# The first projection right after the first chunk's states, with the tiles of the other chunks in its rounds

## The reference, cut to what matters

```python
x = x + attn(cond(x, itok, W), ...)           # x: 32 x 64 x 1024, so 2048 tokens of 1024
x = x + ffn(cond2(x, ...), ...)
# cond:  states[b] = W[itok[b]].T @ x[b]       W: 16 matrices of 64 x 64, one picked for each of 32 sequences
# attn:  q, k, v = states @ ((qw - 8) * repeat(scales, 128, axis=0))     q: 32 heads, k and v: 8, of 128
#        rotary embedding of q and k, causal softmax, context, output projection (also 4-bit weights)
# cond2: two small layers with weights picked by session; ffn: a dense layer + top-2 of 8 low-rank experts
```

## Time and profile before

| | us |
|---|---|
| median of 3 runs | 1913.29 (1912.41 to 1917.9) |
| the profiled execution: its time | 1915.91 |
| its span | 1913.9 |
| TensorE busy | 1729.1 (90%) |
| VectorE busy | 1598.4 (84%) |
| ScalarE busy | 1407.5 (74%) |

### The profile page before, as it was taken

One profiled execution on the slowest core, in us unless ns is written; L12 is line 12 of the kernel. 1 busy time (PEld: TensorE's weight loads), 2 busy tenths in 40 slices (PEclk: granted clock), 3 DMA queues, 4 the chain that ended last, 5 costly groups with the idle time before them and its releaser, 6 DMA issues. The chain is left out here.

```text
span 1913.9 us, 38885 instructions
## 1 busy us (share of the span) xinstructions
PE 1729.1 (90%) x14314; PEld 937.1 (49%) x14314; DVE 1598.4 (84%) x2715; ACT 1407.5 (74%) x2372; POOL 61.3 (3%) x50
## 2 busy tenths in 40 slices
PE   3668999998999899999999998999999978899998
PEld 3424545554554445445544554554544545455553
DVE  5589999999899898989998998899999987556642
ACT  2557988888898888888888888898888775233420
POOL 0200000000000000000000000000000011111100
PEclk8789999999999999999999999999999999899999
DMA  6321030011102010301021012102013111100001
GB/s 212 101 88 46 12 67 23 24 34 47 46 2 72 9 46 1 78 3 46 14 66 29 20 36 45 46 2 74 5 55 101 52 50 55 67 23 34 23 34 44
DMA packets 118582, 87.66 MB, mean 46 GB/s; under 512 B 11996, under 2 KB 110692, under 8 KB 118372
## 3 DMA queue, kind: packets, MB, share of 16 engines
q1 hardware_dynamic: 117732, 84.76, 14.9%
q10 hardware_dynamic: 640, 0.13, 0.0%
HBM read 76.49 MB, written 8.39 MB: 44 GB/s over the span
## 5 line engine op out<-in xcount | busy, mean ns | idle before, releaser
L1311 ACT ACTIVATE pj<-pj,ratio 128x512 f32<-128x512 f32 x865 | 575.4, 684 | 120.0 <-PE pj L1645 114.6
L1643 PE MATMUL pj<-hid,wts 128*128 128x512 f16 x1024 | 392.8, 384 | 66.8 <-DVE pj L826 25.0
L1645 PE MATMUL pj<-hid,wts 128*128 128x512 f16 x1024 | 390.9, 382 | 0.0
L1320 ACT ACTIVATE sbk<-sbk,wts 128x512 f32<-128x512 f32 x384 | 261.8, 682 | 24.2 <-PE sbk L1712 18.9
L1320 ACT ACTIVATE sa<-sa,wts 128x512 f32<-128x512 f32 x384 | 260.8, 679 | 15.6 <-PE sa L1712 15.5
L1643 PEld LDWEIGHTS pj<-hid,wts 128*128 128x128 f16 x1024 | 99.8, 97 | 235.8 <-ACT pj L1311 71.3
L1655 PEld LDWEIGHTS tp<-wts,hid 128*128 128x128 f16 x3072 | 181.7, 98 | 32.5 <-issue 3.5
L1655 PE MATMUL tp<-wts,hid 128*128 128x128 f16 x3072 | 192.5, 219 | 0.5
L1645 PEld LDWEIGHTS pj<-hid,wts 128*128 128x128 f16 x1024 | 100.7, 98 | 77.3 <-issue 1.4
L726 DVE SCALAR_TENSOR_TENSOR work<-pj,ratio,cos_t 128x512 f32<-128x512 f32 x128 | 95.7, 748 | 44.5 <-PE pj L1645 35.5
L1311 ACT ACTIVATE ex<-ex,ratio 128x512 f32<-128x512 f32 x193 | 127.9, 663 | 4.1 <-PE ex L1645 1.6
(11 more groups left out here) (247 smaller groups left out, 3090.4 us busy)
## 6 DMA issues: line engine op xcount, KB each, us to landing
wts<-qo_d SPq DMA_DIRECT2D x64, 256.0 KB, 3.2
y<-x_d SPq DMA_DIRECT2D x7, 2048.0 KB, 7.8
wts<-qq_d SPq DMA_DIRECT2D x35, 256.0 KB, 3.2
int_even<-qq_d SPq DMA_DIRECT2D x29, 256.0 KB, 3.0
out_d<-y SPq DMA_DIRECT2D x12, 512.0 KB, 2.6
work<-qv_d SPq DMA_DIRECT2D x16, 256.0 KB, 7.7
work<-sv_d SPq DMA_DIRECT2D x16, 256.0 KB, 9.4
work<-wb_d SPq DMA_DIRECT2D x8, 512.0 KB, 4.1
```

The costliest lines, as they stand in the source:

```text
L1311: act.activation(unit_bank[u][:, :], unit_bank[u][:, :], ACT.Copy, scale=ratio[:, KT * u + j:KT * u + j + 1]).then_inc(u_scaled[u], 1)
L1320: act.activation(out_bank[t % 2][:, :], out_bank[t % 2][:, :], ACT.Copy, scale=o_ratio[:, REP * t + h:REP * t + h + 1]).then_inc(o_scaled[ ...
L1643: mm(bank[:, :], w_int[:, u, j, :], hid[:, 0, j, CH * c:CH * (c + 1)], start=j == 0, stop=False, skip_group_check=True)
L1645: mm(bank[:, :], w_int[:, u, j, :], hid[:, 1, j, CH * c:CH * (c + 1)], start=False, stop=True, skip_group_check=True).then_inc(u_done[u], 1)
```

## The change

The states of chunk 0 are made as before (its eighth tile in the bank `cx0`, not in a `pj`). Then the 24 rounds of the first projection start, and each holds one tile of the states of the other chunks: round r has tile 8 + r, so chunk 1 stands in rounds 0 to 7, chunk 2 in 8 to 15, chunk 3 in 16 to 23. These tiles go round in four banks (`cx1`, `sa`, `sbk`, `cx0`), since the units hold the other three. ScalarE has the high half behind the rescales of the round, and its integer conversions spread over rounds; two dequantizing operations stand in round 10. VectorE has in the rounds: the low half, maximum and scale of chunk 2 at round 5 and of chunk 3 at round 13, the ropes of three units at rounds 8, 12 and 16, the dequantizing at round 10, and four maxima of w_base at rounds 20 to 23; the fourth rope, the score factors and the other maxima come behind. The maximum of chunk 1 now stands behind the low halves of chunk 0 and the ratios. SP loads the four small tables right after x of chunk 1, and the value weights after the integers of chunk 1. VectorE waits for the small tables at round 8, TensorE after the rounds.

```diff
@@ -318,12 +318,11 @@
             return ((lambda part: w2h[:, part, :], w2_t, col(SC2 + 2)),
                     (lambda part: wrh[:, part, :, :].rearrange("p k e -> p (k e)"), small[:, 256:320], col(SC2 + 1)))
-        cond_banks = [pj[0], pj[1], ex, cx[0], cx[1], sa, sbk]
-        cond_banks = [pj[0], pj[1], ex, cx[0], cx[1], sa, sbk]
+        cond_first = [pj[0], pj[1], ex, cx[0], cx[1], sa, sbk, cx[0]]
+        cond_later = [cx[1], sa, sbk, cx[0]]
         def cond_bank(n):
-            return cond_banks[n % len(cond_banks)]
+            return cond_first[n] if n < KT else cond_later[n % 4]
         def ctx_src(e):
             return cx[e][:, :].rearrange("p (m s) -> p m s", s=SEQ)
@@ -423,12 +422,13 @@
                     load_x(c + 1)
                 if c == 0:
                     load_scales(0)
+                    for dst, src in ((cos_t, rope_cos), (sin_t, rope_sin), (mask_t, neg_mask), (id16, ident16)):
+                        sp.dma_start(dst[:, :], src).then_inc(S["consts_in"], 16)
+                if c < len(INT_BATCHES):
+                    load_first_ints(c)
+                if c == 1:
                     load_piece(0, 0)
                     load_piece(0, 1)
-                if c < len(INT_BATCHES):
-                    load_first_ints(c)
-            for dst, src in ((cos_t, rope_cos), (sin_t, rope_sin), (mask_t, neg_mask), (id16, ident16)):
-                sp.dma_start(dst[:, :], src).then_inc(S["consts_in"], 16)
             load_out_scales(0)
             load_wo(0, 0)
             load_wo(0, 1)
@@ -649,27 +649,22 @@
             dve.wait_ge(S["w_scales_ready"], 1)
             chunk_max(0)
             chunk_scale(0)
-            for c in range(NC):
-                for k in range(KT):
-                    n = c * KT + k
-                    if k == (KT // 4 if c == 0 else 0) and c + 1 < NC:
-                        chunk_max(c + 1)
-                    dve.wait_ge(S["cond_hi"], n + 1)
-                    t = slice(CH * c, CH * (c + 1))
-                    dve.scalar_tensor_tensor(out=hid[:, 1, k, t], in0=cond_bank(n)[:, :], scalar=col(SH + c),
-                                             in1=hid[:, 0, k, t], op0=ALU.mult, op1=ALU.subtract).then_inc(S["cond_split"], 1)
-                if c == 0:
-                    scales_inverted(0)
-                    unit_ratios(0, 0, 3)
-                    unit_ratios(0, 3, NU)
-                if c + 1 < NC:
-                    chunk_scale(c + 1)
-                if c == 0:
-                    dequant_scale(0, 0)
-                    dequant_scale(0, 1)
-                    dequant_split(0, 0)
-                    dequant_split(0, 1)
+            def cond_lo(n):
+                c, k = n // KT, n % KT
+                t = slice(CH * c, CH * (c + 1))
+                dve.wait_ge(S["cond_hi"], n + 1)
+                dve.scalar_tensor_tensor(out=hid[:, 1, k, t], in0=cond_bank(n)[:, :], scalar=col(SH + c),
+                                         in1=hid[:, 0, k, t], op0=ALU.mult, op1=ALU.subtract).then_inc(S["cond_split"], 1)
+            for n in range(KT):
+                cond_lo(n)
+            scales_inverted(0)
+            unit_ratios(0, 0, 3)
+            unit_ratios(0, 3, NU)
+            chunk_max(1)
+            chunk_scale(1)
             def score_factors():
                 link(dve.tensor_scalar(col(A, NC), col(ISH, NC), 1.0 / QKV_DOWN, None, ALU.mult))
@@ -967,8 +962,6 @@
                 dve.wait_ge(S["base_done"], n + 1)
                 dve.scalar_tensor_tensor(out=x1_part(n), in0=base_bank[n % 2][:, :], scalar=col(F_BASE + n // YT), in1=x1_part(n),
                                          op0=ALU.mult, op1=ALU.add).then_inc(S["result"], 1)
-            dve.wait_ge(S["consts_in"], 64)
             def step(p4, ahead, out4, between, pieces):
@@ -1172,17 +1165,41 @@
                     else:
                         step((g, c), (g, c + 1) if c + 1 < NC else (g + 1, 0), None if first and c == 0 else (g, c - 1), between, pieces)
-            score_factors()
-            for u in range(NU - 1):
+            def first_rope(u):
                 rope_cos((0, 0), u)
                 rope_sin((0, 0), u)
                 rope_add((0, 0), u)
                 if u in (0, 1, 2):
                     rope_high((0, 0), u)
                 rope_split((0, 0), u)
-                for k in (2 * u, 2 * u + 1):
-                    dve.wait_ge(wb_in[k % 2], 16 * (k // 2 + 1))
-                    absmax(wbmax[:, k:k + 1], wb_stage[k % 2]).then_inc(S["wb_read"], 1)
+            def wb_max(k):
+                dve.wait_ge(wb_in[k % 2], 16 * (k // 2 + 1))
+                absmax(wbmax[:, k:k + 1], wb_stage[k % 2]).then_inc(S["wb_read"], 1)
+            for r in range(ROUNDS):
+                if r == 8:
+                    dve.wait_ge(S["consts_in"], 64)
+                cond_lo(KT + r)
+                if r == 5:
+                    chunk_max(2)
+                    chunk_scale(2)
+                if r == 10:
+                    dequant_scale(0, 0)
+                    dequant_scale(0, 1)
+                    dequant_split(0, 0)
+                    dequant_split(0, 1)
+                if r == 13:
+                    chunk_max(3)
+                    chunk_scale(3)
+                if r in (8, 12, 16):
+                    first_rope(r // 4 - 2)
+                if r >= 20:
+                    wb_max(r - 20)
+            score_factors()
+            first_rope(3)
+            for k in range(4, WB_STATS):
+                wb_max(k)
             dve.wait_ge(S["wb_read"], WB_STATS)
             dve.reduce_max(stat[:, T_WB:T_WB + 1], wbmax, X).then_inc(S["stat_wb"], 1)
             small_stats()
@@ -1287,20 +1304,18 @@
                 with act.Fori(CT * c, CT * (c + 1)) as i:
                     load_cond(act, i, 1, c)
-            for c in range(NC):
+            def cond_high(n):
+                c, k = n // KT, n % KT
                 act.wait_ge(S["h_scale_ready"], c + 1)
-                for k in range(KT):
-                    n = c * KT + k
-                    act.wait_ge(S["cond_done"], n + 1)
-                    act.activation(hid[:, 0, k, CH * c:CH * (c + 1)], cond_bank(n)[:, :], ACT.Copy,
-                                   scale=col(SH + c)).then_inc(S["cond_hi"], 1)
-                act.wait_ge(S["w_scales_ready"], 1)
-                if c == 0:
-                    for i in range(PIECES):
-                        dequant_hi(0, i)
-                else:
-                    for p in range(*INT_BATCHES[c - 1]):
-                        first_int(p)
+                act.wait_ge(S["cond_done"], n + 1)
+                act.activation(hid[:, 0, k, CH * c:CH * (c + 1)], cond_bank(n)[:, :], ACT.Copy,
+                               scale=col(SH + c)).then_inc(S["cond_hi"], 1)
+            for n in range(KT):
+                cond_high(n)
+            for p in range(2):
+                first_int(p)
             def rescale(p4, u, j):
@@ -1574,8 +1589,14 @@
                 for u, j in quanta(r):
                     if j < KT - 1:
                         rescale((0, 0), u, j)
-                if r in (22,):
-                    rope_high((0, 0), {22: 3}[r])
+                cond_high(KT + r)
+                if r % 4 >= 2 and r < 16:
+                    first_int(2 + 2 * (r // 4) + r % 4 - 2)
+                if r == 10:
+                    act.wait_ge(S["w_scales_ready"], 1)
+                    dequant_hi(0, 0)
+                    dequant_hi(0, 1)
+            rope_high((0, 0), 3)
             group(0, first=True)
             with act.Fori(1, NKV - 1) as g:
                 group(g)
@@ -1617,17 +1638,18 @@
         def _(pe):
             mm = nc.tensor.matmul
-            for c in range(NC):
-                pe.wait_ge(x_in[c], 16)
-                pe.wait_ge(wc_in[c], 16 * CB)
-                for k in range(KT):
-                    n = c * KT + k
-                    if n >= len(cond_banks):
-                        pe.wait_ge(S["cond_split"], n - len(cond_banks) + 1)
-                    for i in range(CT):
-                        last = mm(cond_bank(n)[:, P * i:P * (i + 1)], y[:, CT * c + i, P * k:P * (k + 1)],
-                                  wc[:, CT * c + i, :], start=True, stop=True)
-                    last.then_inc(S["cond_done"], 1)
+            def cond(n):
+                c, k = n // KT, n % KT
+                if k == 0:
+                    pe.wait_ge(x_in[c], 16)
+                    pe.wait_ge(wc_in[c], 16 * CB)
+                if n >= KT - 1:
+                    pe.wait_ge(S["cond_split"], n - 3)
+                for i in range(CT):
+                    last = mm(cond_bank(n)[:, P * i:P * (i + 1)], y[:, CT * c + i, P * k:P * (k + 1)],
+                              wc[:, CT * c + i, :], start=True, stop=True)
+                last.then_inc(S["cond_done"], 1)
             PARTS = ((0, 0), (0, 1), (1, 0))
@@ -1938,13 +1960,17 @@
                     else:
```

(8 more changed lines are left out.)

## The result

| | before | changed |
|---|---|---|
| median of 12 runs each, us | 1914.52 (1910.45 to 1917.9) | 1907.42 (1904.51 to 1911.57) |
| the profiled execution: time, span, us | 1915.91, 1913.9 | 1907.48, 1905.4 |

The ratio is 0.9969, 95% interval 0.9959 to 0.9978: 5.9 us faster (4 to 8). The medians are 7.1 us apart, the two profiled spans 8.5.

A forecast was written before the change was run, and what follows sets the result against it. The opening's end was taken as the issue of the load of A plus 10.6 us. That issue moves from 117.5 to 109.1, so 1913.3 - 8.4 = 1904.9, called 1905 us; range 1900 to 1913.

The forecast's parts named there:

- What bounds: End of the opening: set by the issue of the load of A plus 10.6 us, not by the projection.
- likeliest: Whole kernel: 5.7 to 11.5 us gained, 1902 to 1907.5 us; chance 62%.
- Part 1, SP's queue: SP's queue: chunk 1's fetch loop near 20, chunk 2's x near 26.5 and loop 39.3; value-weight loads 5 to 8 us.
- Part 2: Before round 1: chunk 1's scale at 33.9, rounds 1 to 7 from 34, TensorE in round 8 by 47.
- Part 3: Rounds 8 to 16: VectorE sets the pace; ScalarE waits for chunk 3's scale until 77.9.
- the unknown of 1.6 us in my sum: One more cold start of TensorE within rounds 10 to 18: gain 1.6 us less.
- Part 4: Rounds 17 to 23: round 20's tile done at 84.1, round 23's at 92.1, TensorE's projection ends near 93.5.
- Part 5: VectorE's leftover factors, fourth rope and maxima: load of A at 109.1 instead of 117.5, 8.4 us earlier.
- The tail: Small tables behind the load of A: still 10.6 us from its issue.
- Cold rounds: Rival: pauses leave TensorE at 1.2 GHz to the rounds' end, load of A 6.5 us later than before, 1920; 12%.
- Later than I count: Rival: VectorE or SP later, load of A at 113 to 118, 1909 to 1914 us; 18%.
- the wait on the rope's tables: Round 8: waiting on the small tables costs nothing; issued near 14, wanted at 54.

The follow-up runs named there:

- e4: Changed kernel with the eleven small tables and two statistics loads issued before the first w_base load; ratio 0.9939 to the kernel before.
- e8: Kernel before with the eleven small tables and two statistics loads issued ahead of the w_base loads; ratio 0.9978.
- e6: Changed kernel with the four value-weight loads ahead of chunk 0's integers again, tables still ahead; ratio 0.9982 to the kernel before.
- e3: Changed kernel with chunk 3's maximum and scale at round 11 and GpSimd's memsets behind the fourth rope's sum; ratio 0.9918 to the kernel before.
- e7: Kernel before with GpSimd's memsets of y moved behind the third rope's high half; ratio 1.0002.
- e2: Changed kernel with chunk 3's maximum and scale at round 11 instead of 13, memsets untouched; ratio 0.9961 to the kernel before.
- e1: Changed kernel with GpSimd's four memsets of y moved behind the fourth rope's sum; ratio 0.9938 to the kernel before.
- e5: Changed kernel with cos, sin, mask and identity loaded behind chunk 3's fetch loop again; ratio 1.0052 to the kernel before.

## Why the prediction was right, point by point

*What bounds.* Right: the end of the opening is the issue of the load of A plus a fixed tail. It moved by 7.9 us, the scores by 8.1, the span by 8.5. e4 and e8 shorten the tail and gain 0.3 and 0.2% by it. The measured time also lies at the edge of what I called likeliest (1902 to 1907.5).

*Part 1, SP's queue.* Loop of chunk 1 forecast near 20, measured 21.01; x of chunk 2 near 26.5, measured 26.81; loop of chunk 2 at 39.3, measured 37.53. From x to the loop of chunk 2 it is now 10.7 us, where it was 5.8: the four value-weight loads cost 4.9 us there, and not the 7 of my sum, just below my 5 to 8. In the profile of e6 the rest of the chain hangs on such a shift.

*Part 2.* Chunk 1's scale at 33.4 against 33.9, and TensorE at round 8 by 47.6 against 47. One round was misread: the rescale for round 1 stands ahead of that scale in ScalarE's queue (it ran at 27.42), so round 2, and not round 1, is the first that waits. It changed nothing behind.

*Part 3.* The first low half of chunk 2 was there at 53.0, not 55.4: chunk 2 was 1.6 us earlier, and TensorE's clock stayed up over its pause of 2.65 us before it (tile of 1.13 us at 50.22, not 2.05). That was luck, for in e3 it fell over a pause of 2.63 us at the same place. The wait at round 12 was 3.08 us instead of 1.6, since here TensorE ran at half clock (0.50 in 60:63) behind its pause of 4.42 us; ScalarE, which ended that pause, had itself waited 2.94 us for VectorE's dequantizing. A cold start there was the unknown of 1.6 us in my sum. ScalarE waited for chunk 3's scale as said, to 76.7 against 77.9.

*Part 4.* Here a term was missing: **the cast of the third rope waited 4.2 us for GpSimd's memsets**. I had left GpSimd's queue out of the change because the diff doesn't touch it, though the reduction that its memsets stand behind moved by 12.6 us. Round 20's tile, which needs nothing of that cast, was done at 83.2 (84.1 forecast); round 21's waited 2.87 us, round 23's was done at 94.3 and not 92.1, and TensorE's projection ended at 95.6, not 93.5.

*Part 5.* The first score factor's 2.17 us, which I kept as a possible stall of that place, was the same wait and went away (e7): 2.0 us less. It went away by 0.27 us, the time from the fourth memset's end (97.86) to the factor (98.13); in e2 and e4 the two met and it cost 0.8. Against the forecast the memsets added 4.2 us and round 12's wait 1.5; chunk 2 took off 2.4, the factor 2.0, and the rest some 0.8. So the load of A came out within 0.5 us of the forecast, but by sizes that cancel: e1, without the missing term, has it 3.7 us ahead of the forecast. That the number is this close is luck; what bounds the opening, and which waits replace which, was read rightly.

*The tail* was 10.4 us (109.63 to 120.00) against 10.6. The wait before the scores was forecast as one of about 25 us; it came as 6.22 and 16.29 us with three quanta between them.

*The rivals.* Cold rounds: from round 4 on the clock was at 0.50, that is 1.2 GHz, once, from 60 to 66, and 1.00 through the last rounds. That this hangs by little is shown by e4. The Trainium skill (TensorE: Matmul & The Clock Gate, "HAM oscillation — how this bites in real kernels") describes this pattern; the trace agrees in kind (0.50 in 60:63, behind the pause of 4.42 us), but the end did not shift past the kernel before: the stretch added 1.5 us to VectorE's wait at round 12, and in e4 the cold rounds cost about 1.1 us of the issue of A. Later than I count: e6 and e5 build such cases; e5 shows that the wait on the rope's tables, which I costed at nothing, is nothing only because of their early issue.

## What to carry to other kernels

When a reduction, a scale or any other link moves, follow every queue that hangs on it, also the ones whose code is untouched: a filler on another engine moves along and can meet an operation that it blocks. A gain inside a phase arrives at the end only as far as the longest queue shrinks; here TensorE's projection ended 21 us earlier (95.6 instead of 116.7) and the scores came 8 us earlier. Two further gains of 0.3% each were cheap: one wait that moves the memsets (e1), and small loads issued before they are wanted (e4), in the tail and not in the phase that was rebuilt.

## What the runs showed of the hardware

A VectorE cast from float32 to float16 in SBUF, or a `tensor_scalar` on four columns, took longer while a GpSimd memset ran and ended 0.02 to 0.3 us after the last memset in the row: 4.63 us (memsets to 86.08, cast to 86.36; the same in e4, e5 and e6), 5.94 us (77.86, 78.14; e2), 2.17 us (82.87, 82.89; the same in e8), against 0.43 and 0.16 us with none beside it (e1, e7). The cast of 81.73 stayed out until the last of the memsets of 75.60 to 86.08 was over, though by an estimate of 3.49 us each (10.48 us for three) one of the three ended within it. `scalar_tensor_tensor` and `tensor_tensor` (0.75 and 0.69 us right ahead of the long cast) and `tensor_scalar` on one column (0.15 us) ran beside the same memsets at their usual times, and so did `tensor_reduce` beside e1's (1.22 us at 104.14). The Trainium skill (SBUF — State Buffer, "SBUF: two separate sides") has the rule: VectorE in a two-port mode and GpSimd share a port pair as an exclusive lock, and the one that comes second blocks fully. The trace agrees that the operations above were held up until a memset's end; it shows more than one memset waited for in a row, and no run shows which mode the operations were in.

TensorE's clock after a pause: it fell around the pause of 4.42 us (56.6 to 61.0; granted 0.88 in 57:60, 0.50 in 60:63) and stayed up over those of 3.34, 2.87 and 2.65 us in the changed kernel. It fell in e4 behind a pause of 2.87 us at the same place (0.50 in 87:93) and in e3 behind one of 2.63 us (0.50 in 51:54). So the length of the pause alone doesn't tell which way it goes; a forecast for such a place should carry both.
